# Graph attention on one core: all 17 jobs of a graph through a ring of two PSUM banks, K taken by DVE, four heads of scores in SBUF

## The chip, the cores and the metric

The kernel runs on one core of one Trainium2 chip. The metric is the device time of one launch in microseconds (us); lower is better. Five engines of the core work side by side: PE (matrix products and transposes), ACT (activations, here also copies out of PSUM), DVE (vector work), POOL, and SP, which issues the transfers. Each executes its own program in order and waits on semaphores.

## The reference, cut to what matters

32 graphs of 256 nodes with 384 features, 12 heads of 32 features. For each graph:

```python
q, k, v = heads(x @ Wq + bq), heads(x @ Wk + bk), heads(x @ Wv + bv)
scores = q @ k.T / sqrt(32) + beta * adj            # per head, 256 x 256
scores = where(adj > 0, scores, -9e15)
out = softmax(scores) @ v                           # heads joined: 256 x 384
result = layernorm(x + out)                         # no scale, no shift
```

All is float32. The three projections are computed at near float32 precision from rounded parts: each operand is split into a high part and a low part (`xt_high`, `xt_low`, `w_high`, `w_low`), and three products of parts are added.

## The kernel before, in words

The program is written out for all 32 graphs, by hand, in a software pipeline: while the 12 head steps of graph n run, the projections of graph n+1 and the transposes of x for graph n+2 are slipped in between. In step h (the functions `batch` of each engine):

- PE turns the probabilities of head h (`turn`, four transposes into `t_bank`). At h = 2, 6, 10 it first computes four heads of scores at once (`scores`, into `s_bank0..3`), those used next. At these steps it also multiplies a finished group of four heads with v (`values`, `o_bank`, left half), and two steps later transposes the joined heads back (`turn_group`, `o_bank`, right half). At the end of nearly each step comes one *job* (`project`).
- A job is one of eleven: Q or K of one of three groups of four heads (nine matmuls of 256 columns), V of one of two node tiles (nine matmuls of 384 columns), or X, a transpose of a third of x (two matmuls). All jobs pass through one bank, `j_bank`. ACT empties it (`high`); for X, DVE too, which subtracts the high part (`low`) to get `xt_low`. `free_bank` makes PE wait until the previous job was taken.
- DVE adds the mask and takes the row minimum of the negated scores two heads ahead (`maxima`, two instructions of 128x256 per head), copies two of three turned heads to SBUF (`copy_turned`), divides the group outputs (`divide`), and does small layer-norm work. ACT takes the exponentials one head ahead (`exps`), copies every third turned head, and takes jobs and groups.
- POOL makes the bias of the next graph, adds the residual and normalises. It works alongside and its output is used graphs later.

`neg_scores` and `probs` hold three heads (`NH = 3`). The time of a stretch is set by the in-order queues of PE, ACT and DVE and by who waits for which bank.

Before the first step (the start) PE transposes x of graph 0 into three banks (`first_bank`: `j_bank` and the two `t_bank`s), and then does all eleven jobs of graph 0 and 1's X through `j_bank`.

Of the kernel before, what the change touches and what calls it, by code (L numbers as in the profile page):

```python
# [31 lines left out]
def graph_attention_program(nc, x, adj, wq, bq, wk, bk, wv, bv, beta, out):  # L33
# [7 lines left out]
    STEPS = H  # L41
    NH = 3
    NT = 2
    NP = 8

    JOB = [(kind, g) for kind in "QK" for g in range(G)] + [("X", 0), ("V", 0), ("X", 1), ("V", 1), ("X", 2)]
    JOBS = len(JOB)
    assert JOBS == 2 * G + T + C
    V_DONE = JOB.index(("V", T - 1))
    LOWS = C  # L50
    KV = 2 * G
    EXPS = T * H
    PAIRS = B // 2
# [6 lines left out]
    with ctx:  # L60
# [5 lines left out]

# [26 lines left out]
        heads_t = sb("heads_t", [P, N])  # L93
# [24 lines left out]
        s_bank = [bank(f"s_bank{n}") for n in range(J)]  # L118
# [4 lines left out]
        first_bank = [j_bank, *t_bank]  # L123
        assert len(first_bank) == C
# [9 lines left out]
        w_low_ready = sem("w_low_ready")  # L134
        scores_ready = sem("scores_ready")
        turned = sem("turned")
        group_ready = sem("group_ready")
        group_turned = sem("group_turned")
        job_ready = sem("job_ready")
        max_ready = sem("max_ready")  # L140
        probs_t_v = sem("probs_t_v")
        probs_t_a = sem("probs_t_a")
        low_ready = sem("low_ready")
        high_ready = sem("high_ready")
        exp_ready = sem("exp_ready")
        heads_t_ready = sem("heads_t_ready")
        inv_ready = sem("inv_ready")
        att_ready = sem("att_ready")
        not_edge_ready = sem("not_edge_ready")
        stats_ready = sem("stats_ready")  # L150
        moments_ready = sem("moments_ready")
        half_ready = sem("half_ready")
# [3 lines left out]
        y_ready = sem("y_ready")  # L156
        var_ready = sem("var_ready")
        chain = sem("chain")
# [3 lines left out]
        passed_v, passed_p, passed_s = sem("passed_v"), sem("passed_p"), sem("passed_s")  # L162
        CHAIN = 4 * NEWTON + 2

        def count(i, par, each, more):

            return i * (2 * each) + (par * each + more)

        def wait(eng, s, value):

            if not (isinstance(value, int) and value <= 0):
                eng.wait_ge(s, value)  # L172

        def take_wait(eng, s):


            eng.sem_inc(s, 1)

        def is_last(i, par):
            return isinstance(i, int) and i == PAIRS - 1 and par == 1  # L180

        def is_tail(i):
            return isinstance(i, int) and i == PAIRS - 1

        def has_job(i, par, k):

            return JOB[k][0] != "X" or not is_last(i, par)

        def has_low(k):
            return JOB[k][0] == "X"  # L190

        def job_count(i, par, k):


            return count(i, par, JOBS, C + (sum(has_job(i, par, n) for n in range(k + 1)) if k >= 0 else k + 1))

        def low_count(i, par, k):

            if k >= 0:
                done = sum(has_job(i, par, n) and has_low(n) for n in range(k + 1))  # L200
            else:
                done = -sum(has_low(n) for n in range(JOBS + k + 1, JOBS))
            return count(i, par, LOWS, C + done)

        def jobs_at(i, par, h):


            if h == -1:
                h, i, par = H - 1, i - 1 + par, 1 - par
            if h == H - 1:  # L210
                return () if is_tail(i) else ((i + 1, par, 0),)
            k = h + 1
            if k >= JOBS or is_last(i, par) or not has_job(i + par, 1 - par, k):
                return ()
# [213 lines left out]
        def _(act):  # L428
# [53 lines left out]
            for k in range(JOBS):  # L482
                high(0, 0, k)
# [334 lines left out]
```

## Time and profile before

| | us |
|---|---|
| Median of three runs | 908.89 (907.76 to 910.2) |
| The profiled execution, whole | 911.03 |
| Its span in the profile | 909.2 |
| PE busy | 816.4 (90% of the span) |
| ACT busy | 623.0 (69%) |
| DVE busy | 575.0 (63%) |
| POOL busy | 413.5 (45%) |

The profile's span begins with the first recorded instruction and ends with the last; some two microseconds of the execution lie outside. A busy share counts an instruction as busy until its modelled end, and matmuls overlap, so PE's own rate is better read from the distance between the starts of two instructions that follow each other. In the timeline, rows of like instructions in a row are merged (x3), and the bracket at the end tells how long the engine was idle before and who released it.

### The profile page before, as it was taken

Reading aid. Unit: us, or ns where it says so; the run is one execution under the profiler, and the core shown is the slowest. Engines: PE = TensorE matmul, PEld = TensorE weight load, DVE = VectorE, ACT = ScalarE, POOL = GpSimd, SP = SyncE. Lnnn points to the kernel's source line nnn. Section 1 sums busy time; section 2 is a strip of 40 time slices with the busy share of each in tenths; the row PEclk is TensorE's granted clock in tenths of the full one; section 3 lists DMA queues with packets and bytes.
Section 4 is the critical chain, followed back from the end, with each engine's and each line's share of the span. In section 5 each row is a group of like instructions: output and inputs, shape, how many; then the busy total and the mean of one; then the engine's idle time right before and its main releaser. Section 6 shows DMA issues by size and latency. Waiting matters only on the chain.

```text
span 909.2 us, 23383 instructions
## 1 busy us (share of the span) xinstructions
PE 816.4 (90%) x7296; PEld 632.9 (70%) x7296; DVE 575.0 (63%) x2295; ACT 623.0 (69%) x2116; POOL 413.5 (45%) x660
## 2 busy tenths in 40 slices
PE   4789999999999999999999999999999999999993
PEld 3677776767777767777777777676777676777771
DVE  2156666766666666667675666675666666666676
ACT  3277777767776767776777777776777676777682
POOL 3022543445543445554345554345554344555353
PEclk9999999999999999999999999999999999999998
DMA  4000010111011111101111101011101011110001
GB/s 147 27 30 31 19 48 31 48 48 48 24 42 31 48 48 48 48 19 46 33 48 48 48 20 47 31 49 47 48 20 47 31 47 48 48 41 25 4 18 52
DMA packets 28537, 37.01 MB, mean 41 GB/s; under 512 B 2560, under 2 KB 28416, under 8 KB 28416
## 3 DMA queue, kind: packets, MB, share of 16 engines
q1 hardware_dynamic: 28416, 35.53, 11.9%
q8 instruction: 60, 0.98, 0.4%
q14 instruction: 61, 0.50, 0.2%
HBM read 22.94 MB, written 12.58 MB: 39 GB/s over the span
## 4 chain that ended last, share of the span: by engine, by line
PE 70%; ACT 19%; issue 6%; DVE 3%; DMA 1%; SPq 0%; ACTq 0%; DVEq 0%
PE j_bank L335 35%; PE s_bank L346 11%; PE o_bank L378 10%; PE t_bank L362 10%; ACT probs L437 8%; ACT qk L450 5%; ACT probs_t L463 3%; PE j_bank L306 3%; ACT v_sb L455 2%; DVE xt_low L528 2%; DMA w_raw<-in_L_gnn_Wv_dram 1%; ACT xt_high L457 1%; PE o_bank L386 1%; DVE neg_scores L521 0%; ACTq L172 0%
## 5 line engine op out<-in xcount | busy, mean ns | idle before, releaser
L437 ACT ACTIVATE probs<-neg_scores,neg_max 128x256 f32<-128x256 f32 x768 | 381.4, 500 | 100.5 <-DVE neg_max L521 100.5
L521 DVE CUSTOM_DVE_ANT_0 neg_scores<-s_bank,bias_sb 128x256 f32<-128x256 f32 x768 | 284.1, 417 | 109.3 <-PE s_bank L346 104.4
L362 PE MATMUL t_bank<-ident,probs 128*128 128x128 f32 x1536 | 237.5, 277 | 3.4 <-ACT probs L437 2.4
L534 DVE COPY probs_t<-t_bank 128x512 f32<-128x512 f32 x256 | 176.3, 689 | 56.6 <-PE t_bank L362 56.6
L362 PEld LDWEIGHTS t_bank<-ident,probs 128*128 128x128 f32 x1536 | 173.8, 140 | 52.9 <-issue 32.1
L437 ACT ACTIVATION_READ_ACCUMULATOR probs<-neg_scores,neg_max 128x1 f32 x768 | 146.6, 191 | 0.0
L335 PE MATMUL j_bank<-xt_high,w_high 128*128 128x256 f32 x576 | 120.7, 318 | 18.8 <-ACT w_high L481 6.3
L450 ACT ACTIVATE qk<-j_bank,qk_bias 128x256 f32<-128x256 f32 x192 | 90.7, 472 | 64.0 <-PE j_bank L335 64.0
L335 PEld LDWEIGHTS j_bank<-xt_high,w_high 128*128 128x128 f32 x576 | 81.7, 192 | 60.1 <-ACT qk L450 35.4
L528 DVE TENSOR_TENSOR xt_low<-j_bank,xt_high 128x256 fp32r<-128x256 f32 x93 | 39.5, 425 | 127.2 <-ACT xt_high L457 127.2
L346 PE MATMUL s_bank<-qk 32*128 32x256 f32 x1536 | 110.0, 400 | 0.1
L756 POOL TENSOR_SCALAR var_eps<-mean_var 128x2 f32<-128x2 f32 x31 | 6.0, 193 | 224.0 <-DVE mean_var L575 224.0
L774 POOL TENSOR_SCALAR o_sb<-y_sb,rstd,shift 128x384 f32<-128x384 f32 x62 | 102.2, 1655 | 9.7 <-POOL shift L768 9.7
L378 PE MATMUL o_bank<-probs_t,v_sb 128*32 128x256 f32 x1536 | 102.8, 385 | 0.8 <-DVE att L550 0.8
L335 PE MATMUL j_bank<-xt_high,w_low 128*128 128x256 f32 x576 | 101.0, 284 | 0.0
L335 PE MATMUL j_bank<-xt_low,w_high 128*128 128x256 f32 x576 | 100.7, 284 | 0.0
L455 ACT ACTIVATE v_sb<-j_bank 128x384 f32<-128x384 f32 x64 | 31.4, 491 | 93.6 <-PE j_bank L335 93.6
L335 PE MATMUL j_bank<-w_high,xt_high 128*128 128x384 f32 x192 | 50.6, 373 | 37.9 <-DVE xt_low L528 37.9
L335 PEld LDWEIGHTS j_bank<-xt_low,w_high 128*128 128x128 f32 x576 | 83.2, 192 | 0.0
L335 PEld LDWEIGHTS j_bank<-xt_high,w_low 128*128 128x128 f32 x576 | 83.1, 192 | 0.0
L346 PEld LDWEIGHTS s_bank<-qk 32*128 32x128 f32 x1536 | 69.4, 184 | 17.2 <-issue 11.0
L463 ACT ACTIVATE probs_t<-t_bank 128x512 f32<-128x512 f32 x128 | 74.3, 581 | 0.5 <-PE t_bank L362 0.5
(58 smaller groups left out, 929.6 us busy)
## 6 DMA issues: line engine op xcount, KB each, us to landing
x_sb<-in_x_dram SPq DMA_DIRECT2D x32, 384.0 KB, 3.3
out_dram<-o_sb SPq DMA_DIRECT2D x31, 384.0 KB, 2.5
adj_sb<-in_adj_dram SPq DMA_DIRECT2D x32, 256.0 KB, 3.6
w_raw<-in_L_gnn_Wq_dram SPq DMA_DIRECT2D x1, 576.0 KB, 5.0
w_raw<-in_L_gnn_Wk_dram SPq DMA_DIRECT2D x1, 576.0 KB, 8.4
w_raw<-in_L_gnn_Wv_dram SPq DMA_DIRECT2D x1, 576.0 KB, 9.9
out_dram<-o_sb SPq DMA_DIRECT2D x2, 192.0 KB, 1.9
bv_row<-in_L_gnn_bv_dram SPq DMA_DIRECT2D x1, 192.0 KB, 4.8
```

Of the source, the lines that this page charges most:

```text
L335: mm = pe.matmul(b[:, 0:n], w, a, start=(m == 0), stop=(m == len(pairs) - 1))
L346: mm = pe.matmul(s_bank[j][:, t * N:(t + 1) * N], qk[rows, par, 0, g, t * P:(t + 1) * P], qk[rows, par, 1, g, :], start=True, stop=True)
L362: mm = pe.transpose(b[:, k * N + t * P:k * N + (t + 1) * P], probs[:, (T * h + t) % (T * NH), k * P:(k + 1) * P], ident[:, :])
L378: mm = pe.matmul(o_bank[HD * j:HD * (j + 1), 0:N], v_sb[:, par, k, h * HD:(h + 1) * HD], probs_t[:, (par * H + h) % NP, k, :], start=(k == ...
L437: nc.scalar.activation(probs[:, slot, :], neg_scores[:, slot, :], ACT.Exp, bias=neg_max[:, par, t, h:h + 1], scale=-1.0, accum_out=row_sum ...
L450: ins = nc.scalar.activation(qk[:, par, q, g, :], b[:, 0:N], ACT.Identity, bias=qk_bias[:, q, g:g + 1])
L455: ins = nc.scalar.activation(v_sb[:, par, t, :], b[:, 0:D], ACT.Identity)
L463: nc.scalar.activation(probs_t[:, (par * H + h) % NP, :, :], t_bank[h % NT][:, :].rearrange("p (k q) -> p k q", k=T), ACT.Identity).then_i ...
L521: nc.vector.tensor_tensor_reduce(neg_scores[:, (T * h + t) % (T * NH), :], s_bank[h % J][:, t * N:(t + 1) * N], bias_sb[:, par, t, :], -1. ...
L528: nc.vector.tensor_tensor(xt_low[:, 1 - par, JOB[k][1], :], j_bank[:, 0:N], xt_high[:, 1 - par, JOB[k][1], :].bitcast(F32), ALU.subtract). ...
L534: nc.vector.tensor_copy(probs_t[:, (par * H + h) % NP, :, :], t_bank[h % NT][:, :].rearrange("p (k q) -> p k q", k=T)).then_inc(probs_t_v, 1)
L774: nc.gpsimd.tensor_scalar(o_sb[:, par, t, :], y_sb[:, t, :], rstd[:, t:t + 1], shift[:, t:t + 1], ALU.mult, ALU.subtract).then_inc(normed, 1)
```

## The change

There are now 17 jobs per graph: the eleven from before, and the multiplication with v (`O`, formerly `values`) and the transpose back (`G`, formerly `turn_group`) of each of the three groups. All take their turn in one ring of two banks (`j_bank0`, `j_bank1`); `o_bank` is gone, and so is the use of the `t_bank`s in the start. Job r waits until job r-2 was taken. A table says which jobs follow the turn of which head:

```diff
+    NH = 4
+    NJ = 2
+    def jobs_of(n, h):
+        jobs = {
+            0: (("Q", 0, n + 1), ("K", 0, n + 1)),
+            1: (("O", 2, n - 1),),
+            3: (("G", 2, n - 1), ("Q", 1, n + 1), ("K", 1, n + 1)),
+            4: (("Q", 2, n + 1), ("K", 2, n + 1)),
+            5: (("O", 0, n),),
+            7: (("G", 0, n), ("V", 0, n + 1), ("X", 0, n + 2)),
+            8: (("V", 1, n + 1), ("X", 1, n + 2)),
+            9: (("O", 1, n),),
+            11: (("G", 1, n), ("X", 2, n + 2)),
+        }.get(h, ())
+    ACT_JOBS, DVE_JOBS = "QVXO", "KXG"
-        o_bank = bank("o_bank")
-        j_bank = bank("j_bank")
+        j_bank = [bank(f"j_bank{n}") for n in range(NJ)]
...
+            def run(job):
+                kind, a, n = job
+                r = place[job]
+                b = j_bank[r % NJ]
+                if r >= NJ:
+                    wait_taken(pe, r - NJ)
```

K is now emptied by DVE with an add of its bias (before: ACT, as Q). ACT takes the first job of a step at the end of that step and the other ones in the next step, between its two exponentials; DVE takes K at the head of the next step, X after its copy, and G at the end:

```diff
+                    s = H * n + h
+                    for job in rest_of(n, h - 1):
+                        if job[0] == "K":
+                            take(job)
+                    if h % J != 2 and s + 2 < B * H:
+                        maxima(s + 2)
+                    if s >= 1 and not by_scalar((s - 1) % H):
+                        copy_turned(s - 1)
+                    for job in rest_of(n, h - 1):
+                        if job[0] == "X":
+                            take(job)
...
+                    for job in first_of(n, h):
+                        take(job)
```

`neg_scores` and `probs` hold four heads, `heads_t` two groups. The start runs its jobs in the order X X X, then Q and K in turn, V V, X X X, through the same ring. The counts of semaphores are computed from the ring in place of closed forms; POOL's and SP's work and order are as before.

On PE, from the turn of head 10 of a graph on, before:

```order
L362 MATMUL t_bank0<-ident,probs 128x128 x4
L378 MATMUL o_bank<-probs_t,v_sb 32x256 x8
L362 MATMUL t_bank1<-ident,probs 128x128 x4
L335 MATMUL j_bank<-xt_high,w_high 128x256 x3
L335 MATMUL j_bank<-xt_low,w_high 128x256 x3
L335 MATMUL j_bank<-xt_high,w_low 128x256 x3
L362 MATMUL t_bank0<-ident,probs 128x128 x4
L386 MATMUL o_bank<-ident,heads_t 128x128 x2
L335 MATMUL j_bank<-xt_high,w_high 128x256 x3
L335 MATMUL j_bank<-xt_low,w_high 128x256 x3
L335 MATMUL j_bank<-xt_high,w_low 128x256 x3
```

and now, from the same place (heads 10 and 11 are the first two rows):

```order
L341 MATMUL t_bank0<-ident,probs 128x128 x4
L341 MATMUL t_bank1<-ident,probs 128x128 x4
L301 MATMUL j_bank1<-ident,heads_t 128x128 x2
L282 MATMUL j_bank0<-ident,x_sb 128x128 x2
L341 MATMUL t_bank0<-ident,probs 128x128 x4
L273 MATMUL j_bank1<-xt_high,w_high 128x256 x3
L273 MATMUL j_bank1<-xt_low,w_high 128x256 x3
L273 MATMUL j_bank1<-xt_high,w_low 128x256 x3
L273 MATMUL j_bank0<-xt_high,w_high 128x256 x3
L273 MATMUL j_bank0<-xt_low,w_high 128x256 x3
L273 MATMUL j_bank0<-xt_high,w_low 128x256 x3
```

What moved: the multiplication with v no longer stands here, the last X (L282) now stands one short turn ahead of the first Q of the next graph, and Q and K follow each other without a turn between them.

On DVE, before, around the `xt_low` of the last X of a graph (it is followed by the maxima of the next graph's first heads):

```order
L575 BN_AGGR mean_var<-stats 128x2 x2
L534 COPY probs_t<-t_bank1 128x512
L528 TENSOR_TENSOR xt_low<-j_bank,xt_high 128x256
L521 ISA neg_scores,neg_max<-s_bank0,bias_sb 128x256
L521 ISA neg_max 128x1
L521 ISA neg_scores,neg_max<-s_bank0,bias_sb 128x256
L521 ISA neg_max 128x1
L521 ISA neg_scores,neg_max<-s_bank1,bias_sb 128x256
L521 ISA neg_max 128x1
L521 ISA neg_scores,neg_max<-s_bank1,bias_sb 128x256
L521 ISA neg_max 128x1
```

and now, from the maxima of the second head (`s_bank1`) of the next graph on:

```order
L440 ISA neg_scores,neg_max<-s_bank1,bias_sb 128x256
L440 ISA neg_max 128x1
L440 ISA neg_scores,neg_max<-s_bank1,bias_sb 128x256
L440 ISA neg_max 128x1
L462 TENSOR_TENSOR att<-j_bank0,inv_sum 128x2x128
L440 ISA neg_scores,neg_max<-s_bank2,bias_sb 128x256
L440 ISA neg_max 128x1
L440 ISA neg_scores,neg_max<-s_bank2,bias_sb 128x256
L440 ISA neg_max 128x1
L472 COPY probs_t<-t_bank1 128x512
L455 TENSOR_TENSOR xt_low<-j_bank1,xt_high 128x256
```

What moved: `xt_low` of the last X stood ahead of the maxima of heads 0, 1 and 2; now it stands behind them, behind a division (`att`) and a copy.

On PE, the start of the program, before:

```order
L306 MATMUL j_bank<-ident,x_sb 128x128 x2
L306 MATMUL t_bank0<-ident,x_sb 128x128 x2
L306 MATMUL t_bank1<-ident,x_sb 128x128 x2
L335 MATMUL j_bank<-xt_high,w_high 128x256 x3
L335 MATMUL j_bank<-xt_low,w_high 128x256 x3
L335 MATMUL j_bank<-xt_high,w_low 128x256 x3
L335 MATMUL j_bank<-xt_high,w_high 128x256 x3
L335 MATMUL j_bank<-xt_low,w_high 128x256 x3
L335 MATMUL j_bank<-xt_high,w_low 128x256 x3
```

and now:

```order
L282 MATMUL j_bank0<-ident,x_sb 128x128 x2
L282 MATMUL j_bank1<-ident,x_sb 128x128 x2
L282 MATMUL j_bank0<-ident,x_sb 128x128 x2
L273 MATMUL j_bank1<-xt_high,w_high 128x256 x3
L273 MATMUL j_bank1<-xt_low,w_high 128x256 x3
L273 MATMUL j_bank1<-xt_high,w_low 128x256 x3
L273 MATMUL j_bank0<-xt_high,w_high 128x256 x3
L273 MATMUL j_bank0<-xt_low,w_high 128x256 x3
L273 MATMUL j_bank0<-xt_high,w_low 128x256 x3
```

What moved: the third transpose of x goes into the bank of the first, and each job of nine matmuls uses the other bank than the one before it.

## Rows read from the trace of the kernel before

**Rows 1.** Windows view: stretch and length, then each engine's busy us, PEclk, DMA.

```profile
16.30:30.50 14.20, 11.42 (x45) 9.97 (x45) 1.60 (x2) 2.33 (x5) 6.34 (x4) 1.00 0.15 46
391.25:418.24 26.99, 25.12 (x232) 19.48 (x232) 17.67 (x72) 19.29 (x67) 13.14 (x21) 1.00 0.12 40
```

**Rows 2.** Waits view, 48 to 880 us: who waited for whom, us, times, longest.

```profile
PEld j_bank L335 <- ACT xt_high L457: 42.1, 30, 1.4
...
PEld j_bank L335 <- ACT qk L450: 30.5, 93, 0.4
```

**Rows 3.** Timeline of PE in one graph: start, length, line, tiles, [idle before].

```profile
413.12 0.44 PE L306 MATMUL j_bank<-ident,x_sb 128*128 128x128 f32 x2
413.39 0.60 PE L362 MATMUL t_bank<-ident,probs 128*128 128x128 f32 x4
...
415.41 0.76 PE L335 MATMUL j_bank<-w_high,xt_high 128*128 128x384 f32 x3 [1.19 <-DVE xt_low L528]
...
417.06 0.60 PE L362 MATMUL t_bank<-ident,probs 128*128 128x128 f32 x4
...
418.17 1.15 PE L346 MATMUL s_bank<-qk 32*128 32x256 f32 x16
419.25 0.66 PE L362 MATMUL t_bank<-ident,probs 128*128 128x128 f32 x4
419.83 1.07 PE L378 MATMUL o_bank<-probs_t,v_sb 128*32 128x256 f32 x16
420.83 0.66 PE L362 MATMUL t_bank<-ident,probs 128*128 128x128 f32 x4
421.24 0.60 PE L335 MATMUL j_bank<-xt_high,w_high 128*128 128x256 f32 x3
...
422.39 0.60 PE L362 MATMUL t_bank<-ident,probs 128*128 128x128 f32 x4
```

**Rows 4.** Timeline of DVE in the same graph.

```profile
414.83 0.42 DVE L528 TENSOR_TENSOR xt_low<-j_bank,xt_high 128x256 fp32r<-128x256 f32 x1 [2.17 <-ACT xt_high L457]
...
416.32 0.69 DVE L534 COPY probs_t<-t_bank 128x512 f32<-128x512 f32 x1
416.92 0.42 DVE L550 TENSOR_TENSOR att<-o_bank,inv_sum 128x256 f32<-128x256 f32 x1
...
419.51 0.42 DVE L521 CUSTOM_DVE_ANT_0 neg_scores<-s_bank,bias_sb 128x256 f32<-128x256 f32 x1
...
419.86 0.42 DVE L521 CUSTOM_DVE_ANT_0 neg_scores<-s_bank,bias_sb 128x256 f32<-128x256 f32 x1
```

**Rows 5.** Timeline of ACT in the same graph.

```profile
413.46 0.50 ACT L437 ACTIVATE probs<-neg_scores,neg_max 128x256 f32<-128x256 f32 x1
...
413.95 0.58 ACT L463 ACTIVATE probs_t<-t_bank 128x512 f32<-128x512 f32 x1
414.43 0.38 ACT L457 ACTIVATE xt_high<-j_bank 128x256 fp32r<-128x256 f32 x1
414.69 0.51 ACT L437 ACTIVATE probs<-neg_scores,neg_max 128x256 f32<-128x256 f32 x1
```

**Rows 6.** Timeline of PE in the start of the kernel.

```profile
12.76 1.01 PE L335 MATMUL j_bank<-xt_high,w_high 128*128 128x256 f32 x3 [6.30 <-ACT w_high L481]
...
16.30 1.01 PE L335 MATMUL j_bank<-xt_high,w_high 128*128 128x256 f32 x3 [1.14 <-ACT qk L450]
...
17.75 0.84 PE L335 MATMUL j_bank<-xt_high,w_low 128*128 128x256 f32 x3
...
41.51 0.44 PE L306 MATMUL j_bank<-ident,x_sb 128*128 128x128 f32 x2 [0.58 <-ACT v_sb L455]
41.88 1.15 PE L346 MATMUL s_bank<-qk 32*128 32x256 f32 x16
```

**Rows 7.** Timeline of ACT in the start of the kernel.

```profile
11.55 2.22 ACT L481 ACTIVATE w_high<-w_raw 128x1152 fp32r<-128x1152 f32 x2 [4.67 <-DVE qk_bias L633]
```

**Rows 8.** Timeline of DVE in the start of the kernel.

```profile
11.42 0.42 DVE L636 TENSOR_TENSOR xt_low<-j_bank,xt_high 128x256 fp32r<-128x256 f32 x1
```

More of the change, by code:

```diff
@@ L179, in is_last @@
[L179 to L203, printed above, removed]
@@ L338, in scores, with values @@
-            def scores(i, par, g):
-                wait(pe, high_ready, job_count(i, par, G + g))
-                wait(pe, max_ready, count(i, par, EXPS, T * J * g))
+                    mm = pe.transpose(b[:, t * P:(t + 1) * P], x_sb[:, n % 2, t, c * P:(c + 1) * P], ident[:, :])
+                return mm
+            def values(g, n, b):
+                wait_copied(pe, H * n + J * (g + 1))
+                if g == 0:
+                    wait(pe, taken_a, act_taken[place["V", T - 1, n] + 1])
+                for k in range(T):
+                    for j in range(J):
+                        h = J * g + j
+                        mm = pe.matmul(b[HD * j:HD * (j + 1), 0:N], v_sb[:, n % 2, k, h * HD:(h + 1) * HD],
+                                       probs_t[:, (H * n + h) % NP, k, :], start=(k == 0), stop=(k == T - 1))
+                return mm
@@ new lines, in turn_heads @@
+            def turn_heads(g, n, b):
+                wait(pe, taken_a, act_taken[place["O", g, n] + 1])
+                for t in range(T):
+                    mm = pe.transpose(b[:, t * P:(t + 1) * P], heads_t[:, (G * n + g) % 2, t * P:(t + 1) * P], ident[:, :])
+                return mm
+            def run(job):
[4 more added lines that the diff above has]
+                    wait_taken(pe, r - NJ)
+                if kind == "X":
+                    mm = turn_x(a, n, b)
+                elif kind == "O":
+                    mm = values(a, n, b)
+                elif kind == "G":
+                    mm = turn_heads(a, n, b)
+                else:
+                    mm = project(kind, a, n, b)
+                mm.then_inc(job_ready, 1)
@@ L343, in scores @@
+            def scores(n, g):
+                wait_taken(pe, place["K", g, n])
+                wait(pe, max_ready, T * (H * n + J * g))
                 for t in range(T):
@@ L427, in _ @@
+            for job in last_jobs:
+                run(job)
         @block.scalar
         def _(act):
-            def exps(i, par, h):
-                for t in range(T):
-                    wait(act, max_ready, count(i, par, EXPS, T * h + t + 1))
-                    if t == 0:
-                        wait(act, turned, count(i, par, STEPS, h - NH + 1))
-                    slot = (T * h + t) % (T * NH)
-                    nc.scalar.activation(probs[:, slot, :], neg_scores[:, slot, :], ACT.Exp,
-                                         bias=neg_max[:, par, t, h:h + 1], scale=-1.0,
-                                         accum_out=row_sum[:, par, t, h:h + 1]).then_inc(exp_ready, 1)
@@ L663, in batch @@
[L663 to L675 removed]
+            for job in first_jobs[C:-C]:
+                take(job)
```

633 lines of the change are left out of this document (272 added, 361 removed).

## Prediction

> **What bounds the kernel now.** I read the page's first part, then the windows view, the waits of PE's weight loads, and the timelines of PE, DVE and ACT over one graph, and last the start. In the stretch from one graph's first scores to the next, 26.99 us, PE is busy for 25.1, ACT for 19.3 and DVE for 17.7 [rows 1]: the loop goes by PE, and what can be won is PE's waiting and nothing else. PE's pure work, from the distance between starts [rows 3]: scores 1.08 us (418.17 to 419.25), three times; a turn 0.58 behind scores (419.25 to 419.83), three times, else 0.41 (420.83 to 421.24), nine times; values 1.00 (419.83 to 420.83), three times; Q or K 1.15 (421.24 to 422.39), six times; V 1.65 (415.41 to 417.06), twice; X 0.27 (413.12 to 413.39), three times; the transpose of a group, two matmuls like X, 0.27, three times. That is 3.24 + 1.74 + 3.69 + 3.00 + 6.90 + 3.30 + 0.81 + 0.81 = 23.5 us. So 3.5 us of each graph are not pure work. Most of them are waits for the single job bank: 42.1 us in 30 waits for the X that ACT and DVE both take, 30.5 in 93 for a Q or K that ACT takes [rows 2]; the first kind ends with the 1.19 us idle ahead of 415.41 [rows 3]. Over some 31 graphs these two are 2.3 us each time; waits of X for the same bank are of the same kind. I leave 0.45 of the 3.5 as changes between kinds of matmul, an estimate, and keep it in the new sum.
>
> **The waits for a free bank go.** With two banks a Q that ends is taken while K runs for 1.15 us. ACT's take costs some 0.5 with its handover, DVE's the same (its `xt_low` took 0.58 from start to PE's next, 414.83 to 415.41 [rows 3, 4]). K on DVE is an operation that the trace does not show (one PSUM operand, 128x256): from below by 0.35, the pitch of a maximum of that shape 419.51 to 419.86 [rows 4], from above by 0.60, a copy twice as large (416.32 to 416.92); I take 0.35, the same columns. Three per graph add about 1.05 us to DVE, which is free for over 9 of 27, and take about as much from ACT. Neither sets the end by its sum.
>
> **New waits, walked from the start of the next graph's first scores (time 0).** Each is the later of two chains.
> - Q behind the last X. DVE: first maximum at 1.34 (418.17 to 419.51 [rows 3, 4]), three heads of maxima of 2 x 0.345 = 2.08, the division of a group (0.35, same shape), a copy 0.60, `xt_low` with its release 0.58: 4.95. PE is there after 1.08 + 0.58 + 0.41 + 0.27 + 0.27 + 0.41 = 3.02. Wait 1.93. This was a wait of 1.2 before, for another job; the order of DVE makes it longer.
> - The turn of head 3. ACT must first take O (which blocks it until PE has finished O, some 0.15 to 0.2 after the next start), then two exponentials of 0.49 (413.46 to 413.95 [rows 5]), then copy head 1 (0.48, 413.95 to 414.43; with release 0.6). With the take at 0.26 (414.43 to 414.69): 0.15 + 0.26 + 0.98 + 0.65 = 2.04, against 1.66 of PE. Wait 0.38.
> - The first X behind G: two heads of maxima from 1.34 (1.38), a copy 0.60, a `bn_stats` counted like a maximum (0.35), the division with its release 0.58: 4.25, against 1.08 + 0.58 + 0.41 + 0.27 + 1.65 = 3.99. Wait 0.26.
> - Scores of groups 1 and 2 must find their banks read: K's take (0.2 + 0.35), two maxima (0.70) and 0.15 of handover are 1.40, against turn and values, 1.41. I count 0.1 for both together.
>
> Sum 2.67; the period is 23.5 + 0.45 + 2.67 = 26.6 us, 0.4 less than now. Behind the waiting Q stand K and the next turns on PE; ACT and DVE work ahead in that time, so nothing further is delayed. Bounds: waits per graph from 1.4 (only a wait like the 1.19 of now) to 3.6 (K's take at the copy's 0.60 delays both later groups of scores by 0.25, and the two small waits are 0.25 larger). Some 30 graphs run in this loop: 30 x 0.4 = 12 us. The fourth slot of `neg_scores` and `probs` is worth nothing here: DVE was not waiting for exponentials in the loop. POOL, SP and the transfers keep their work and have slack of microseconds.
>
> **The start.** Now the first Q begins at 12.76 and the first scores at 41.88 [rows 6], over eight projections and three X. A Q took from 16.30 to 17.75 + 0.84 = 18.59, of which about 0.2 is drain, so 2.1 us against 1.15 in the loop: the merged row of three matmuls has 1.01 us there and 0.60 in the loop [rows 3, 6]. The granted clock is recorded as 1.00 in both stretches [rows 1], so the record doesn't show it; by the durations, a factor of 1.8, I read the lower level, 1.2 GHz, in the start and 2.4 GHz from about 41 us on, where the X took 0.44 (41.51). Before it rose PE had run one job at a time with gaps between them, 1.14 the first [rows 6]; it rose near the end of the last V.
> - Lost: the third X now needs the first bank, which DVE takes only at 11.42 [rows 8] (it waits for the small inputs). So X is done at about 12.6, ACT takes it until 13.0, and its rounding of the weights starts there, not at 11.55 [rows 7]; the first Q starts at 14.2, 1.45 later.
> - Won: from there eight projections without a gap. Two of Q and K at 2.1 lead to 18.4, where I assume the clock to rise (the bounds are at once, 2 us better, and never, a rival below); one of 1.8, three of 1.15 and two V of 1.65 lead to 27.0. X X X with one wait for both takes (1.2) end at 29.0, where the scores start: 12.9 earlier than 41.88.
>
> The Trainium skill bears on this: TensorE: Matmul & The Clock Gate, "The HAM clock gate", says that the half-rate clock is the default and that sustained matmul work releases it. That agrees with the start's 2.1 us per Q, though this trace's clock record does not show the step.
>
> The first graph's steps, the one graph without X and the end change by about +1, -0.5 and -0.6; I count them as zero.
>
> **Sum.** Against the profiled execution, 911.03: 911.03 - 12.9 - 12 = 886.1. That execution is 2.1 above the median of the runs, so 884.
>
> **The rivals.**
> - The clock does not rise in the start (0.13). For it: no stretch of the start with work at that density shows it; against it, the rise in the last V. Six jobs of 2.1, two V of 3.0 and slower X bring the scores to 35.2, a gain of 6.7: 890.
> - The small waits vanish and the long one shrinks (0.15), if the first maximum comes sooner than 1.34 after the scores or DVE overlaps better than the pitches say. Waits of 2.1 make the period 26.0; 30 x 1.0 = 30: 866. Speaks for it: I added worst cases one by one. Against: each of the three chains is in program order.
> - The loop gains nothing (0.10): one handover more of 0.4 per graph that I missed, such as a late K. Period 27.0: 896.
> - Slower by DVE's order (0.04): K's take stands at the head of DVE's step and blocks the maxima behind it until PE is done with K; then scores, exponentials and turns all come later. It decides once waits pass 3.6 per graph. At 3.8 the period is 27.8, 30 x 0.8 = 24, less the start 12.9: 920.
> - Slower by the clock (0.03). PE then waits 1.93 at one place, longer than any wait of now in the loop, where the record stays at 1.00 with waits of 1.19 [rows 1, 3]. If each such wait brought the lower level for the Q and K behind it, that is 2 x (2.1 - 1.15) = 1.9 per graph, 57 in all: 884 + 57 = 941. The same page of the Trainium skill, "A second HAM failure mode: psum-queue depth-cycling", speaks against this change by that rule: cycling through banks gives short idle times after which the clock swings. By the rule the loop would be in that state already; the trace disagrees so far.
>
> **How the numbers follow.** The forecast, 884, has 0.55. Its own range is 874 to 893: plus or minus 0.25 us of waits per graph (7.5) and 3 of the start. The range for 8 in 10 reaches to the cases of 890 and 866 and to the 896 at its upper end: 866 to 897. A measurement of this kernel tells 0.3% (2.7 us) from no change. Faster takes in the forecast and the first three rivals, 0.93; the two slower cases hold 0.07, of which 0.02 falls within 0.3%.
>
> **What would show it.** In the profile after: first scores at 29 us (35 with a low clock); a period of 26.6 between first scores; one long wait per graph of PE for `xt_low` on DVE (1.5 to 2 us) and short ones for ACT's copy behind O; no waits of Q or K for a bank; K on DVE at about 0.42 each. I would be wrong if PE waited for DVE's K at the scores, if the wait of Q were well under a microsecond, or if the granted clock fell in the loop.

## The result, and the profile after

The changed kernel takes 875.0 us (median of three runs, 874.11 to 879.13) against 908.89 (907.76 to 910.2): a ratio of 0.964, with a 95% interval of 0.959 to 0.969. The profiled execution took 875.0, its span is 873.2. Ratios leave out one execution, of experiment 3, that took 885.1 us at a mean granted clock of 0.975, where its others had 0.984 to 0.989.

The first part of the page, which answers to the busy rows of the table before:

```profile
PE 769.3 (88%) x7296; PEld 624.9 (72%) x7296; DVE 610.8 (70%) x2391; ACT 592.8 (68%) x2020; POOL 415.4 (48%) x660
...
L452 DVE TENSOR_SCALAR qk<-j_bank,qk_bias 128x256 f32<-128x256 f32 x96 | 46.4, 484 | 153.4 <-PE j_bank L273 153.4
```

DVE is busy for 36 us more than before and ACT for 30 less. The second row is the operation that the trace of before did not show: K on DVE, 484 ns each, and DVE stood idle for 153.4 us ahead of it, so it had time for it.

The start, timeline of PE (start, length, line, tiles, how long idle before and who released it), beside [rows 6]:

```profile
10.07 0.66 PE L282 MATMUL j_bank<-ident,x_sb 128*128 128x128 f32 x2 [4.78 <-DVE xt_low L455]
12.46 0.98 PE L273 MATMUL j_bank<-xt_high,w_high 128*128 128x256 f32 x3 [1.72 <-ACT w_high L404]
...
15.79 0.81 PE L273 MATMUL j_bank<-xt_high,w_low 128*128 128x256 f32 x3
16.43 0.53 PE L273 MATMUL j_bank<-xt_high,w_high 128*128 128x256 f32 x3
...
23.86 0.38 PE L282 MATMUL j_bank<-ident,x_sb 128*128 128x128 f32 x2
24.61 0.44 PE L282 MATMUL j_bank<-ident,x_sb 128*128 128x128 f32 x2 [0.36 <-ACT v_sb L383]
25.43 0.41 PE L282 MATMUL j_bank<-ident,x_sb 128*128 128x128 f32 x2 [0.39 <-DVE xt_low L455]
25.77 1.15 PE L328 MATMUL s_bank<-qk 32*128 32x256 f32 x16
```

The third X waits for DVE's take, as foreseen. But that take came sooner than in the trace of before, because the small inputs that DVE waits for had landed sooner. Its first instruction, before and now:

```profile
10.68 0.76 DVE L632 TENSOR_SCALAR w_raw<-w_raw 128x1152 f32<-128x1152 f32 x1 [10.68 <-DMA beta_col<-in_L_gnn_beta_dram]
```

```profile
8.76 0.76 DVE L550 TENSOR_SCALAR w_raw<-w_raw 128x1152 f32<-128x1152 f32 x1 [8.76 <-DMA beta_col<-in_L_gnn_beta_dram]
```

Over the thirteen profiles of this case, whose first transfers are the same, this instruction starts between 8.39 and 10.68 us. So 1.9 us of what the start gained is chance and not the change.

From 12.46 on no projection has a bracket: they follow each other without a gap. A row of three matmuls starts 0.64 after the one before it until 16.43, and 0.35 after it from 16.80 on. That step is TensorE's clock going from the lower level (1.2 GHz) to the upper (2.4 GHz), although the granted clock is recorded as 1.00 throughout. The first scores start at 25.77; they started at 41.88, and with inputs as late as then they would start at about 27.7 (an estimate from these rows; experiment 3, with the inputs at 10.56, has them at 27.20).

One graph, timeline of PE, from one graph's first scores to the next one's. It answers to [rows 3]:

```profile
391.10 1.15 PE L328 MATMUL s_bank<-qk 32*128 32x256 f32 x16
392.17 1.13 PE L341 MATMUL t_bank<-ident,probs 128*128 128x128 f32 x8
393.14 0.38 PE L301 MATMUL j_bank<-ident,heads_t 128*128 128x128 f32 x2
393.36 0.38 PE L282 MATMUL j_bank<-ident,x_sb 128*128 128x128 f32 x2
394.59 0.63 PE L341 MATMUL t_bank<-ident,probs 128*128 128x128 f32 x4 [0.84 <-ACT probs L370]
396.01 0.58 PE L273 MATMUL j_bank<-xt_high,w_high 128*128 128x256 f32 x3 [0.80 <-DVE xt_low L455]
...
399.66 1.15 PE L328 MATMUL s_bank<-qk 32*128 32x256 f32 x16
...
401.74 0.63 PE L341 MATMUL t_bank<-ident,probs 128*128 128x128 f32 x4 [0.35 <-issue]
...
413.04 0.41 PE L282 MATMUL j_bank<-ident,x_sb 128*128 128x128 f32 x2 [0.28 <-issue]
...
417.07 1.15 PE L328 MATMUL s_bank<-qk 32*128 32x256 f32 x16
```

From 391.10 to 417.07 is one whole graph, 25.97 us; the undisturbed graphs take 26.04 in the mean, against 27.02 before (26.99 in the one of [rows 1]). Only four rows have a bracket. The two long ones lie 1.4 us apart: the turn at 394.59 and the Q at 396.01, which starts 4.91 us after the scores. Who they wait for is read on the other engines, in the next graph, DVE first:

```profile
418.41 0.43 DVE L440 CUSTOM_DVE_ANT_0 neg_scores<-s_bank,bias_sb 128x256 f32<-128x256 f32 x1 [0.44 <-PE s_bank L328]
...
419.80 0.42 DVE L462 TENSOR_TENSOR att<-j_bank,inv_sum 128x256 f32<-128x256 f32 x1
...
420.82 0.69 DVE L472 COPY probs_t<-t_bank 128x512 f32<-128x512 f32 x1
421.42 0.41 DVE L455 TENSOR_TENSOR xt_low<-j_bank,xt_high 128x256 fp32r<-128x256 f32 x1
```

and ACT:

```profile
418.88 0.51 ACT L370 ACTIVATE probs<-neg_scores,neg_max 128x256 f32<-128x256 f32 x1 [0.31 <-DVE neg_max L440]
...
419.88 0.57 ACT L394 ACTIVATE probs_t<-t_bank 128x512 f32<-128x512 f32 x1
```

DVE's chain is the one that was walked: maxima, division, copy, `xt_low`. ACT's was not walked: the first turn of a new graph (PE, 420.56) starts as ACT ends its copy of head 10 (419.88 + 0.57 and a handover). The bracket names an exponential because the copy and the exponentials are on one engine; the exponentials of that head had ended at 419.88.

The waits view, 48 to 850 us (total us, times, longest), the lines of PE beside [rows 2]:

```profile
PE t_bank L341 <- ACT probs L370: 27.1, 32, 1.1
PE j_bank L273 <- DVE xt_low L455: 24.2, 30, 0.9
PE t_bank L341 <- issue: 10.9, 31, 0.4
PE j_bank L282 <- issue: 8.6, 28, 0.4
```

No Q, K or V waits for the take of a job before it any more; four waits per graph remain, 2.3 us by their brackets.

A last thing was not there before: in three of thirty stretches of 26 us the granted clock is 0.93 (all were 1.00 before). Windows view of one of them, stretch and length, busy us of PE, PEld, DVE, ACT, POOL, then PEclk:

```profile
414.00:440.00 26.00, 24.02 (x221) 19.88 (x220) 17.72 (x69) 17.36 (x61) 13.16 (x21) 0.93 0.14 42
```

and what it is on PE, right behind the two long waits:

```profile
420.56 0.63 PE L341 MATMUL t_bank<-ident,probs 128*128 128x128 f32 x4 [0.84 <-ACT probs L370]
421.98 0.59 PE L273 MATMUL j_bank<-xt_high,w_high 128*128 128x256 f32 x3 [0.80 <-DVE xt_low L455]
...
422.86 0.84 PE L273 MATMUL j_bank<-xt_high,w_low 128*128 128x256 f32 x3
```

The rows of three take 0.84 again, until the multiplication with v at 426.26, which takes its usual 1.07. That graph runs from 417.07 to 444.63, 27.56 us in place of 26.04.

**Where the time went.** The spans differ by 36.0. The first scores come 16.1 earlier (41.88 to 25.77), of which 1.9 is the earlier landing. The first graph takes 23.31 against 25.09 (-1.8). The next thirty take 785.3 against 807.4 (-22.1): 29 of them at 26.04 for 27.02 (-28.4), the one without X at 25.5 for 23.9 (+1.6), and the three falls of the clock (+4.7). The end, from the last graph's scores, takes 38.8 against 34.8 (+4.0): nothing is left there to put between the turns, and their waits stand bare. PE's brackets in that stretch add up to 7.6 (the longest 1.21) against 4.2 before, and the clock falls once more in it: behind a bracket of 0.99 a multiplication with v takes 1.94 in place of 1.07. -16.1 - 1.8 - 22.1 + 4.0 = -36.0.

### The profile page after: what moved, and what is told of

Its sections match the earlier page's. It is cut to its first block, busy times and chain, and to the rows that moved or that the text cites. A ratio compares the mean times of both kernels' runs of the same rounds, so it can differ in the third digit from the quotient of the medians.

```text
span 873.2 us, 23363 instructions
## 1 busy us (share of the span) xinstructions
PE 769.3 (88%) x7296; PEld 624.9 (72%) x7296; DVE 610.8 (70%) x2391; ACT 592.8 (68%) x2020; POOL 415.4 (48%) x660
## 4 chain that ended last, share of the span: by engine, by line
PE 80%; DVE 10%; issue 7%; ACT 1%; DMA 1%; DVEq 0%; SPq 0%; ACTq 0%
PE j_bank L273 25%; PE t_bank L341 16%; PE s_bank L328 12%; PE j_bank L270 12%; PE j_bank L293 11%; DVE neg_scores L440 4%; DVE probs_t L472 2%; PE j_bank L282 2%; PE j_bank L301 2%; DVE xt_low L455 1%; DVE neg_max L440 1%; DMA beta_col<-in_L_gnn_beta_dram 1%; ACT probs L370 1%; DVEq L430 0%; ACT w_high L404 0%
## 5 line engine op out<-in xcount | busy, mean ns | idle before, releaser
L341 PE MATMUL t_bank<-ident,probs 128*128 128x128 f32 x1536 | 231.0, 280 | 43.6 <-ACT probs L370 29.4
L341 PEld LDWEIGHTS t_bank<-ident,probs 128*128 128x128 f32 x1536 | 169.0, 141 | 93.9 <-ACT probs L370 89.5
L452 DVE TENSOR_SCALAR qk<-j_bank,qk_bias 128x256 f32<-128x256 f32 x96 | 46.4, 484 | 153.4 <-PE j_bank L273 153.4
L273 PE MATMUL j_bank<-xt_high,w_high 128*128 128x256 f32 x576 | 110.1, 300 | 26.0 <-DVE xt_low L455 24.2
L381 ACT ACTIVATE qk<-j_bank,qk_bias 128x256 f32<-128x256 f32 x96 | 45.7, 476 | 124.1 <-PE j_bank L273 124.1
L273 PEld LDWEIGHTS j_bank<-xt_high,w_high 128*128 128x128 f32 x576 | 82.1, 192 | 34.0 <-ACT xt_high L385 30.5
L293 PE MATMUL j_bank<-probs_t,v_sb 128*32 128x256 f32 x1536 | 103.7, 388 | 1.2 <-DVE probs_t L472 1.2
L387 ACT ACTIVATE heads_t<-j_bank 128x256 f32<-128x256 f32 x96 | 36.9, 384 | 60.1 <-PE j_bank L293 60.1
L617 POOL TENSOR_SCALAR adj_beta<-adj_sb,beta_col 128x512 f32<-128x512 f32 x32 | 66.2, 2067 | 12.4 <-DMA adj_sb<-in_adj_dram 12.4
```

The costliest lines, as they stand in the source:

```text
L273: mm = pe.matmul(b[:, 0:N], wp[:, q, c, a * P:(a + 1) * P], xp[:, n % 2, c, :], start=(m == 0), stop=(m == 3 * C - 1))
L293: mm = pe.matmul(b[HD * j:HD * (j + 1), 0:N], v_sb[:, n % 2, k, h * HD:(h + 1) * HD], probs_t[:, (H * n + h) % NP, k, :], start=(k == 0), ...
L341: mm = pe.transpose(b[:, k * N + t * P:k * N + (t + 1) * P], probs[:, (T * s + t) % (T * NH), k * P:(k + 1) * P], ident[:, :])
L452: ins = nc.vector.tensor_scalar(qk[:, n % 2, 1, a, :], b[:, 0:N], qk_bias[:, 1, a:a + 1], None, ALU.add)
L617: nc.gpsimd.tensor_scalar(adj_beta[:, :, :], adj_sb[:, n % 2, :, :], 0.0, beta_col[:, 0:1], ALU.max, ALU.mult).then_inc(adj_beta_ready, 1)
```

## The experiments

Each was run in three rounds beside the kernel before on the same chip, whose medians were 910.5 for the first four, 908.9 for the next four and 910.3 for the last three. Ratios are against that. The changed kernel's own ratio is 0.964, and only intervals that lie apart are read as a difference.

### 1. The second bank in the start

The theories: my start (no gaps, so the clock rises early) against one in which the gaps alone are saved and the clock goes its own way.

```diff
-                if r >= NJ:
+                if 1 <= r < len(first_jobs):
+                    wait_taken(pe, r - 1)
+                elif r >= NJ:
                     wait_taken(pe, r - NJ)
```

> The changed kernel with one difference: during the start (the first 14 jobs) each job waits until the one just before it was taken, as with a single bank; the loop is as changed. Theory (the start gained because unbroken work lets the clock rise early, and because no job waits for its bank): the gaps of about 0.75 us per job are back, the matmuls stay at 0.84 us per three until late in the start, the first scores come at 38 to 42 us instead of 25.8, and the time is 12 to 16 us longer than the changed kernel, 887 to 891. Rival (the gain of the start is the gaps alone, or inputs that happened to land 2 us earlier): the clock rises early all the same, first scores at 31 to 33, 6 to 8 us longer, 881 to 883.

Measured: 893.6 us, ratio 0.983 (0.978 to 0.987), 19 us slower than the changed kernel. PE's timeline in the start:

```profile
19.11 1.01 PE L273 MATMUL j_bank<-xt_high,w_high 128*128 128x256 f32 x3 [0.56 <-ACT qk L383]
...
39.39 1.16 PE L270 MATMUL j_bank<-w_low,xt_high 128*128 128x384 f32 x3
...
45.12 2.09 PE L330 MATMUL s_bank<-qk 32*128 32x256 f32 x16
```

A gap of 0.56 to 0.62 stands behind each job, and the clock does not rise before the first scores: the last row of V takes 1.16 (0.69 in the changed kernel), the scores 2.09 (1.15). The profiled execution is the slowest of the four (900.4; the others took 891.5 to 894.8).

The first scores come 19.4 later. 3.4 of it lie ahead of the first Q: 1.7 because the small inputs were there at 10.51 and not at 8.76, which is chance, and 1.7 because the third X waits for one take more. The other 15.9 I split from start to start, since a bracket counts from the modelled end and so leaves out a part of the gap. Without a gap a Q or K takes 1.92 at the lower clock (14.51 to 16.43 in the changed kernel) and 1.06 at the upper; with its gap it takes 2.8 to 2.9 here (3.2 the first), and a V 3.8 for 2.88 (three rows 0.96 apart). The gaps are 9.2 of the 15.9, those between the X included; the other 6.8 are the lower clock. It stays low into the first graph, which takes 26.1 for 23.3. So the gaps are not all that a dense start saves: the clock is 6.8 us up to the first scores, and the first graph's 2.8 come with it. This is shown. 893.6 is somewhat above what I gave, because even the V, the X and the first scores ran at the lower clock.

### 2. The second bank in the loop

The same edit for all jobs behind the start.

```diff
-                if r >= NJ:
+                if r >= len(first_jobs):
+                    wait_taken(pe, r - 1)
+                elif r >= NJ:
                     wait_taken(pe, r - NJ)
```

> The changed kernel with one difference: after the start each job waits until the one just before it was taken, so the ring works as one bank, with the jobs where the change put them. Theory (the second bank is what makes the pairs of jobs possible): K waits for Q's take (0.55, three times), Q1 for the division of G (1.1), V0 for that of G (1.7), X for V (0.6, twice), V1 and O for xt_low (about 1), so some 6 to 8 us per graph, a period of 32 to 34 and a time of 1055 to 1115 us. Rival (the spread of jobs over the steps is what gains, the bank little): period below 27, time below 905.

Measured: 1171.2 us, ratio 1.287 (1.284 to 1.290), slower than I gave. PE, one graph:

```profile
399.88 1.15 PE L330 MATMUL s_bank<-qk 32*128 32x256 f32 x16
...
404.19 0.76 PE L270 MATMUL j_bank<-w_high,xt_high 128*128 128x384 f32 x3 [1.89 <-issue]
...
436.04 1.15 PE L330 MATMUL s_bank<-qk 32*128 32x256 f32 x16
```

This graph takes 36.2 us; the mean is 35.8. With one bank, jobs placed in a row wait for a take each (0.54 to 0.58), and a V behind a G that DVE divides only at the end of its step waits 1.89. Rows at the lower clock appear behind such waits. So the new order of jobs needs the second bank; the two can't be priced apart. That the kernel before managed with one job bank because its order puts a turn ahead of nearly every job is argued; no run has the old order with two banks.

### 3. Who takes K

```diff
-    ACT_JOBS, DVE_JOBS = "QVXO", "KXG"
+    ACT_JOBS, DVE_JOBS = "QKVXO", "XG"
```

> The changed kernel with K emptied by ACT with an activation, between its two exponentials of the next step, and DVE left with X and G. Theory (neither ACT nor DVE is the bound, so who takes K matters little as long as it is a bank ahead): within 4 us of the changed kernel, 871 to 879; the long wait of the first Q and the wait of the turn of head 3 stay. Rival 1 (the move of K to DVE is a part of the gain): one us more per graph on ACT shows, 900 or more. Rival 2 (K at the head of DVE's step delays maxima): faster by 0.1 to 0.2 per graph, 869 to 872.

Measured: 874.2 us (871.2 to 885.1), ratio 0.960 (0.956 to 0.964): no difference from the changed kernel. Its waits view has the same two long waits:

```profile
PE t_bank L341 <- ACT probs L370: 26.8, 32, 1.1
PE j_bank L273 <- DVE xt_low L456: 24.2, 30, 1.0
```

DVE is busy for 44.5 us less (566.3) and ACT for 44.5 more (637.3), and PE's waits are the same. K on DVE costs and brings nothing: the undisturbed graphs take 26.01 here and 26.04 in the changed kernel, so the rival that K delays the maxima by 0.1 to 0.2 per graph falls too.

### 4. The last X two steps earlier

If the chain up to `xt_low` sets the start of the Q, an X ahead of the scores should free it.

```diff
-            9: (("O", 1, n),),
-            11: (("G", 1, n), ("X", 2, n + 2)),
+            9: (("O", 1, n), ("X", 2, n + 2)),
+            11: (("G", 1, n),),
```

> The changed kernel with the last X of a graph moved from behind the turn of head 11 to behind the multiplication with v at head 9, two steps earlier. Theory (the first Q waits 2.0 us because xt_low of that X stands behind three heads of maxima, a division and a copy on DVE): that wait is gone; what is left ahead of the first Q is the wait of the turn of head 0 (until 3.5 us after the scores), and X itself waits 0.3 for its bank. 0.7 to 0.8 us less per graph, about 22 us, and no fall of the clock behind that wait any more (another 5): 845 to 855 us. Rival (the wait only moves, because the turn of head 0 and ACT's queue set the pace there): less than 0.3 us per graph, 866 or more, and the clock still falls.

Measured: 859.4 us (858.9 to 860.2), ratio 0.944 (0.942 to 0.946): 15.6 us faster, half of what I gave per graph (25.68 in the mean against 26.04). PE:

```profile
410.46 0.41 PE L282 MATMUL j_bank<-ident,x_sb 128*128 128x128 f32 x2 [0.23 <-DVE xt_low L455]
410.80 1.15 PE L328 MATMUL s_bank<-qk 32*128 32x256 f32 x16
...
414.28 0.63 PE L341 MATMUL t_bank<-ident,probs 128*128 128x128 f32 x4 [1.09 <-ACT probs L370]
414.66 0.60 PE L273 MATMUL j_bank<-xt_high,w_high 128*128 128x256 f32 x3
```

The Q's wait is gone, and the Q starts 3.86 after the scores in place of 4.91: 1.05 won. But the X had stood inside the turn's wait, where it cost nothing. Ahead of the scores it costs its own 0.22 to 0.34 and a wait of 0.23 for its bank, and the turn's wait grows from 0.84 to 1.09. What is left is 0.4 per graph, 11 us. Most of the rest is the clock: here no stretch of the loop shows it lowered, and the three falls of the changed kernel were 4.7.

### 5. Other heads copied by ACT

The turn of head 3 stands behind ACT's copy of head 1, the first X behind a copy and a division on DVE, and the turn of the new graph behind ACT's copy of head 10. The first two can be moved by giving ACT other heads:

```diff
     def by_scalar(h):
-            return h % 3 == 1
+            return h % 4 == 2
```

> The changed kernel with other turned heads copied by ACT: heads 2, 6 and 10 instead of 1, 4, 7 and 10; DVE copies the other nine. Theory (two of the small waits come from copies that stand in the way: the turn of head 3 waits 0.4 for ACT's copy of head 1 behind O, and the first X waits 0.3 for the division that stands on DVE behind the copy of head 6): both go, 0.6 to 0.7 us per graph, about 20 us less than the changed kernel, 853 to 858; the waits of the turn of head 0 and of the first Q stay. Rival (one copy more on DVE, 0.6 us per graph, lengthens its chain to xt_low and gives it back): 870 or more.

Measured: 844.5 us (844.1 to 845.2), ratio 0.930 (0.928 to 0.931): 30 us faster where I gave about 20. PE's waits:

```profile
PE t_bank L341 <- ACT probs L370: 29.1, 34, 1.1
PE j_bank L273 <- DVE xt_low L455: 24.4, 30, 1.0
```

Both `issue` lines are gone, and with them 0.9 us per graph (25.11 in the mean of the undisturbed graphs); 29 x 0.93 is 27 of the 30. The two went together, so neither is priced alone. The brackets had read 0.35 and 0.28 for these waits, 0.63 together: from start to start they were 0.5 each, and that is what came back.

### 6. Both together

> Both edits: the last X at head 9 and ACT's copies at heads 2, 6, 10. Theory (the waits are separate places in the graph, so they add): 859.4 less about 20, 838 to 842. Rival (they share ACT's or DVE's queue, so only the larger counts): 850 or more.

Measured: 830.7 us (830.1 to 831.3), ratio 0.914 (0.913 to 0.916). The two edits add up (15.6 and 30.5 off 875 would be 829): a graph takes 24.76 in the mean, and before the last two graphs no stretch shows a lowered clock.

### 7. The copy behind which the turn waits

Still the first turn of a new graph waits 1.1 for a copy of head 10. Here ACT copies heads 0, 2, 6 and 8, and DVE takes head 10, ahead of the maxima (added to both edits above):

```diff
-            return h % 4 == 2
+            return h in (0, 2, 6, 8)
...
+                    if h == H - 1:
+                        copy_turned(s - 1)
                     if h % J != 2 and s + 2 < B * H:
                         maxima(s + 2)
-                    if s >= 1 and not by_scalar((s - 1) % H):
+                    if s >= 1 and h != H - 1 and not by_scalar((s - 1) % H):
```

> The last X at head 9; ACT copies heads 0, 2, 6 and 8; and at head 11 DVE copies the turned head 10 ahead of the maxima. Theory (with the X gone, the turn of head 0 starts 3.5 us after the scores because its bank is free only when ACT has copied head 10, behind the exponentials of head 0; with that copy on DVE between the maxima of two heads the turn goes by the exponentials alone, about 3.0): half a us per graph on top of the two small waits, 822 to 832 us. Rival (that wait is for the exponentials, as the profile's releaser says, and DVE's chain gets longer): no better than the version with two edits, 838 or more.

Measured: 823.9 us (823.4 to 824.6), ratio 0.907 (0.905 to 0.909). The wait is 0.70 in place of 1.10, and a graph takes 24.46, 0.3 less where I gave half a us:

```profile
420.69 0.66 PE L341 MATMUL t_bank<-ident,probs 128*128 128x128 f32 x4 [0.70 <-ACT probs L370]
```

This shows that the copy on ACT was the cause of 0.4 of it. Behind it comes the chain of scores, maximum and exponential itself: in the trace the last exponential of head 0 ends at 420.54 and the turn starts at 420.69.

### 8. Three heads of scores in place of four

```diff
-    NH = 4
+    NH = 3
```

> The changed kernel with three heads of scores and probabilities in SBUF (NH = 3), as before the change. Theory (no engine waits for a slot in the loop): the same as the changed kernel, 872 to 880. Rival (the fourth head lets the maxima run ahead and is a part of the loop's gain): 0.3 us per graph or more, 884 and up.

Measured: 872.3 us (871.1 to 873.0), ratio 0.960 (0.958 to 0.961), a graph 26.03 in the mean, as in the changed kernel. The fourth slot is worth nothing in this order.

### 9. A projection inside the wait

If only the chain is left, work that needs nothing of it should fill it: the first Q of the graph after next, ahead of the turn. On top of experiment 7:

```diff
-            0: (("Q", 0, n + 1), ("K", 0, n + 1)),
+            0: (("K", 0, n + 1),),
...
-            11: (("G", 1, n),),
+            11: (("G", 1, n), ("Q", 0, n + 2)),
```

(and the Q of graph 1 at the end of the start).

> The version of e7, and the first Q of the next graph but one moved from behind the turn of head 0 to ahead of it, behind the last G (it reads only x, which has been ready for long); in the start it runs behind the last X. Theory (a wait for the exponentials costs nothing while other work stands ahead of the waiting instruction): the wait of 0.7 to 0.8 us of the turn of head 0 is filled by 1.15 us of Q: 0.7 us per graph, about 22 us, 799 to 806. Rival (PE's time is then no longer the bound, DVE's chain of maxima is, and the wait turns up at the scores): 812 or more.

Measured: 814.2 us (813.8 to 820.0), ratio 0.896 (0.893 to 0.900). PE:

```profile
421.76 0.60 PE L273 MATMUL j_bank<-xt_high,w_high 128*128 128x256 f32 x3
...
422.91 0.60 PE L341 MATMUL t_bank<-ident,probs 128*128 128x128 f32 x4
423.60 0.58 PE L273 MATMUL j_bank<-xt_high,w_high 128*128 128x256 f32 x3
...
424.93 0.63 PE L341 MATMUL t_bank<-ident,probs 128*128 128x128 f32 x4
```

The turn has no wait left, but a graph takes 24.08 for 24.46: 0.38 less, half of the 0.7 that I gave, so it came out near the rival. The rest came back behind the turn, in waits too short for a bracket. The K at 423.60 starts 0.69 after the turn, for 0.41 in experiment 7, and the next turn 1.33 after the K, for 1.15 of a projection behind a turn. DVE, in the same graph, tells what they wait for:

```profile
423.08 0.42 DVE L462 TENSOR_TENSOR att<-j_bank,inv_sum 128x256 f32<-128x256 f32 x1
...
424.10 0.68 DVE L472 COPY probs_t<-t_bank 128x512 f32<-128x512 f32 x1
```

K's bank is free when DVE has divided the last G (423.50), and the next turn starts 0.15 after DVE's copy. So DVE's chain is the next bound here, as the rival said, though the wait turned up at K and not at the scores. The start costs something too: the added Q waits 1.02 us for its `xt_low`, and the first scores behind it take 2.09 us, at the lower clock. (The profiled execution is the slowest of the four, 820.0; the others took 813.8 to 814.6.) This is the best order found, 7% below the changed kernel.

### 10 and 11. The start's wait for the small inputs

DVE takes the first X before it waits for the weights and small inputs, so that the third X gets its bank sooner; once on top of experiment 9, once on the changed kernel alone.

```diff
+            for job in first_jobs[:C]:
+                take(job)
             dve.wait_ge(w_in[0], DMA)
             dve.wait_ge(small_in, 4 * DMA)
...
-            for job in first_jobs[:C]:
-                take(job)
```

> The version of e9, and in the start DVE takes the three X of graph 0 before it waits for the weights and the small inputs. Theory (the third X waits for its bank and so delays the rounding of the weights): the rounding starts when the scaled weights are there, 0.3 to 1.4 us earlier: 0.3 to 1.4 us less than e9. Rival (the weights' landing sets the start): no difference.

> The changed kernel with that edit of the start alone. Same theories: 0.3 to 1.4 us less than the changed kernel, or no difference; the third X then ends before 8 us and the first Q starts within 0.2 us of the end of the first rounding either way.

Measured: 813.9 us (812.1 to 814.9), ratio 0.894 (0.892 to 0.896), on top of experiment 9; 881.0 us (878.7 to 882.3), ratio 0.968 (0.966 to 0.970), alone. The intervals overlap with those of the kernels they are edits of, so neither total shows a difference. In the second one the third X moved from 10.07 to 5.97, but the first Q only from 12.46 to 11.74:

```profile
11.74 0.98 PE L273 MATMUL j_bank<-xt_high,w_high 128*128 128x256 f32 x3 [5.11 <-ACT w_high L404]
```

It waits for ACT's rounding of the weights, and the first scores are at 25.69 against 25.77. The landing hides a part of the gain: the small inputs came at 9.45 us here and at 8.76 there. Counted from the landing the first Q starts after 2.3 us with the edit (experiments 10 and 11) and after 3.7 without it (the changed kernel, experiment 9). In experiments 9 and 10 the inputs landed at the same time (10.56 and 10.55), and the first Q comes 1.41 earlier and the first scores 1.40 (29.51 for 30.91). So the edit does what the theory says, 1.4 us, and the rival of no difference is wrong; it is too little to be seen in the totals. The median of experiment 11 even lies higher, and the profile has a reason that is not in the start: an undisturbed graph takes 26.05, the same, but five graphs have a lowered clock, against three.

## Why the prediction was right, and what was off

It said 884 and faster; it is 875.0. Term by term:

- **What bounds it: right.** PE sets the loop of the changed kernel. Moving 44.5 us between ACT and DVE changed nothing (experiment 3), and PE's waits taken away came back as time (5, 7, and half of it in 9, where DVE's chain begins to set the pace).
- **The start: right in kind, 3.2 too small, and 1.9 of that is luck.** -16.1 for -12.9. The first Q came at 12.46, not 14.2, because the small inputs were there at 8.76 us and not at 10.68. The walk from there was right: 3.7 us from the landing to the first Q, in the changed kernel as in experiment 3 (10.56 to 14.25), where 14.2 less 10.68 makes 3.5. The clock rose 4.0 us after the first Q (at 16.4), assumed was 4.2. That it came so near is luck too: over the eleven profiles with this dense start the rise comes 2.7 to 5.9 after the first Q. From the first Q to the scores it took 13.3 against 14.8: four projections behind the rise took 4.25 (16.43 to 20.68), where I had one of 1.8 and three of 1.15, 5.25 together. That a dense start raises the clock, the assumption without a row, is shown by experiment 1. The rival of a clock that stays low is what that experiment ran into, not this kernel.
- **The waits of the loop: the long one right in sum, two too small.** The Q starts 4.91 after the scores (4.95 was walked). But its wait of 1.93 is in truth two: the turn ahead of it already waits for ACT's copy of head 10, 1.01 from start to start, and the Q for 1.07 more. I had walked DVE's chain and not ACT's; it made no difference to the sum, since the Q's own chain ends later, but it hid the second wait, which experiment 4 then met. The turn of head 3 waits 0.5 (0.38 was given), the first X 0.5 (0.26), the scores nothing (0.1). Together 3.0 against 2.67.
- **The pure work: the term that was mis-sized.** I had 23.5 + 0.45. From start to start between 391.10 and 417.07 it is: scores 3.2, twelve turns 5.5, O 3.0, Q and K 6.6, V 3.4, X 0.7, G 0.5, in all 22.9; with the waits, 3.0, this is the whole 25.97. G is 0.13 to 0.22 and X 0.22 to 0.25 where I gave 0.27 to each, Q with K behind it 2.12 to 2.30 where I gave 2.30. And with each piece read beside its own neighbours nothing is left for the 0.45 "as changes between kinds". What stood there in the kernel before was waits of X for the single bank, which I named and did not count. The waits view of before has them, 48 to 880 us (PEld is PE's weight load):

```profile
PEld j_bank L306 <- ACT v_sb L455: 22.9, 60, 0.4
PEld j_bank L306 <- ACT qk L450: 10.9, 30, 0.4
```

That is 33.8 us, 1.1 per graph. The pure work was 1.0 too much, against 0.35 too little in the waits: the graph takes 26.0, not 26.6, and 29 times 0.56 is 16 us.
- **The loop's clock: a rival that was partly real.** In the changed kernel 3 graphs of 30 lost the upper clock, at 1.5 us each (4.7), not all of them at 1.9 (57). The falls stand behind the pair of long waits. Of the 29 graphs between the first and the last two, the profiles of the kernels with the pair have 3 (changed), 4 (experiment 1), 1 (3), 2 (5), none (8) and 5 (11) with a lowered clock, 15 of 174; those without the Q's wait (4, 6, 7, 9, 10) have none of 145. So in these kernels the falls need the pair, but it is not enough for one, and what decides in which graph the clock falls, and how often, stays open. The mean granted clocks of whole executions agree: those of the changed kernel took 874.1, 875.0 and 879.1 us at mean granted clocks of 0.990, 0.986 and 0.984, and those of experiment 11 have 0.978 to 0.983. The rule that stood with this rival (the Trainium skill, TensorE: Matmul & The Clock Gate, "A second HAM failure mode: psum-queue depth-cycling") agrees with the trace as far as the clock falls behind short idle times, 3 times in 30 graphs; the swing in every graph is not there.
- **The ends: wrong in sign.** The first graph gave 1.8 back, the graph without X took 1.6 more and the end 4.0 more, where I had about +1, -0.5 and -0.6 and counted all as zero. The waits at the last turns are read in the profile; no run tested them, nor why the graph without X lost.

In sum, against the forecast's -24.9 on the span: start -3.2, first graph -1.8, loop -10.1 (-22.1 for -12, with the clock's 4.7 and the 1.6 of the graph without X in it), end +4.0, together -11.1, which makes the -36.0. The misses do not all have one sign: some 16 more than foreseen from the period and 5 from the start and the first graph stand against some 10 lost to the clock, the graph without X and the end. So the total lies nearer to the forecast than its largest part, and that is luck.

## What to carry to other kernels

Take pure work from start to start for each kind *in each neighbourhood*, add it up, and account for the whole period with named waits; the remainder booked here as an overhead of the hardware was a wait not counted. A dense run of matmuls early is worth more than its gaps, because it also brings TensorE's clock up: here 6.8 us beside 9.2 of gaps, and up to 2.8 more in the first graph. When one wait per period is left, look at what stands inside it before moving anything: work in a wait is free, work taken out of it is not, and other work can be put into it, though only as much comes back as the next chain allows (experiments 4 and 9). And before a start is compared between two traces, look when the inputs landed in each.

## What the runs showed of the hardware that was not expected

- The recorded clock does not show the start. It reads 1.00 while rows of three matmuls start 0.64 apart, and the same when they start 0.35 apart. The durations show it.
- In the loop the clock falls now and then, for some 4 us, behind two idle times of 0.84 and 0.80 with one turn between them: in 3 of 30 graphs of the changed kernel, in none to 5 in the others that have the pair. Behind one of 1.09 alone it did not in any of thirty graphs (experiment 4).
- The two waits with brackets of 0.28 and 0.35 us were worth 0.9 together when they went (experiment 5): a bracket counts from the modelled end of the last matmul, not from when PE could have started the next one. Waits of 0.2 to 0.4 can have no bracket at all (experiment 9).
- The same copy-and-add from PSUM costs the same on both engines: Q on ACT takes 476 ns, K on DVE 484.
